# A decoder kernel on one core: a new order for the end of the last batch, a bank and a signal for each slot tile of an expert, and final sums on two engines

## The chip, the core and the metric

The kernel runs on one core of one Trainium2 chip. A core has five engines that each work through their own list of instructions in order and wait for one another by semaphores: TensorE (PE) for matmuls and transposes, VectorE (DVE), ScalarE (ACT), GpSimd (POOL), and SyncE (SP), which here only issues transfers. POOL issues the indirect (scatter) transfers. The metric is the device time of one execution in microseconds (us), as the median of the runs.

## The reference

Everything is float32. The input is x of 4 batches x 512 tokens x 128 features. One decoder layer is computed, with a layer norm after each of three parts:

```
# 1. gated delta net (8 heads, key and value width 128), then a small MLP
q, k = l2norm(silu(h Wq)), l2norm(silu(h Wk));  v = silu(h Wv);  h = rms_norm(x)
S = S * alpha_t ;  S = S + k_t (v_t - k_t S) beta_t ;  o_t = q_t S * scale   # over the 512 tokens
x1 = x + (rms_norm(o) * w * silu(h Wg)) Wo
a  = layernorm(x + x1 + relu(rms_norm(x1) W_fc)^2 W_proj)
# 2. attention of every token to 8 fixed rows of the context
x2 = layernorm(a + attention(a, ctx))
# 3. mixture of 8 experts, 2 for each token, at most 320 tokens to an expert, in token order
gates = softmax(x2 router_w + router_b);  idx = top 2;  pos = cumsum(mask) - 1;  valid = pos < 320
y = sum over the chosen experts of gate * (gelu(x2 w1[e] + b1[e]) w2[e] + b2[e])
out = layernorm(x2 + y)
```

## The kernel before

**Stages.** A prologue loads weights and prepares the keys of batch 0. Then each batch b of 0 to 3 goes through `levels(b)`, eight calls of `step(b, s)` and `between(b)`, which every engine has in its own version. The 512 tokens are four chunks of 128, and the 8 heads are two groups of four, so a batch has 8 units, n = 0 to 7. The recurrence is done in chunk form, for which a triangular system has to be inverted for each chunk and head. `between(b)` holds that inversion for batch b + 1: DVE eliminates 32 x 32 blocks in 31 dependent stages (`eliminate`, lines 1828 to 1860), with two places in it for other work (`aside(18)` and `aside(24)`, lines 1890 to 1896). The blocks then go out to memory and come back in another layout, by transfers on SP (`exchange_t`), and `levels` joins them into 128 x 128 blocks with small matmuls.

**The scan.** `step(b, s)` runs unit s of batch b: TT times v (`scan_tr`, PE), a copy on ACT, the products with the state (`scan_ks`, `scan_qs`, `scan_au`, `scan_ktu`), then on DVE `out_sum` (output of the unit), `state`, `out_norm` (its squared sum), then a power on POOL (`out_power`, line 493), then `gate_out` on DVE one step later (line 1701), and from it `out_transpose` and `out_proj` on PE, which give the residual. For b below 3 the same step prepares the keys of unit s + 2 of the next batch.

**Work of the batch before.** What follows the scan of a batch ("post" work) is cut into pieces: `post_x1`, `post_ssx`, `post_r1`, `post_m` (residual and its rms norm), `post_mT`, `post_fc`, `post_relu2`, `post_y` (MLP), `post_a_stats`, `post_rs1`, `post_a` (norm), `post_aT`, `post_sc`, `post_scores`, `post_sexp`, `post_probs`, `post_pT`, `post_xo` (attention), `post_x2_stats`, `post_rs2`, `post_x2` (norm), `post_x2T`, `post_lg`, `post_logits`, `post_lexp`, `post_choice`, `post_cum`, `post_slots` (router: a slot number for each token and choice), and `post_scatter` (POOL: 2 indirect transfers for each chunk of 128 tokens, line 587). The first ones up to `post_a` stand in `between(b)`; `post_aT` stands in `levels(b + 1)`, the rest in the steps of batch b + 1, and the scatters of batch b, 8 transfers, in POOL's `between(b + 1)`, between the power of the value norms (`rn`, line 547: 128 x 32 elements) and `post_r1(b + 1)`. The order of all of it is written out by hand in each engine's `step`, `post_piece` and `between`.

**The last batch** is split in two parts of two chunks each, FIRST and LAST. FIRST starts in step 5 of batch 3; LAST follows the last unit. The two are interleaved by hand in the branch `if kb >= B` of each engine's `between`. On DVE that is lines 1865 to 1886, on PE 949 to 966, on ACT 1408 to 1419.

**The gates** of the batch after next are 21 small dependent DVE operations on 128 x 32 elements (`gate_op`, lines 1605 to 1646). 3 of them stand early in step 6, the other 18 at its end (line 1801).

**Experts** (lines 1222 to 1240 on PE). SP loads the 320 slots of each expert as three tiles of 128, 128 and 64 rows (SLOT_TILES). For expert e PE transposes the rows, does the first product (4 matmuls into 4 banks), and the second (4 matmuls for each slot tile), with all three tiles in one PSUM bank, 5 or 6 by turns. ACT does the GELU. DVE waits for all three tiles, adds the bias b2, then multiplies by the gate (lines 2144 to 2153); POOL then adds the rows to memory with three accumulating indirect transfers (line 617), into `y_rows` for even experts and `out` for odd ones.

**Final norm** (lines 2155 to 2176). Two transfers for each batch bring both sums in; DVE adds them and takes the statistics, POOL takes the power, DVE the shift, and ACT writes the normalised rows, four instructions for each batch. Two sets of statistics are used by turns, so that DVE's `bn_aggr` of batch i waits for ACT to be done with batch i - 2 (`f_y`).

## Time and profile before

| | |
|---|---|
| median of 3 runs | 739.68 us (737.93 to 739.82) |
| profiled execution, its own time | 743.6 us |
| its span | 741.8 us |
| mean granted PE clock | 0.917 of full speed |
| batches 0 to 3 with what is between them | from 80 to 612 us of the span |
| rest of the last batch | 612 to 660 us |
| experts | 661 to 723 us |
| final norm | 724 to 742 us |

A line of a timeline has the start and the duration in us, engine, line, operation, the tiles written and read, the number of instructions that were merged, and in brackets how long the engine had been idle before and what released it. "issue" means that the profile shows no releaser. Line 470 is a helper for all powers with exponent -0.5, line 632 one for all transposes, line 667 one for products by heads, line 1247 one for copies on ACT; there the tile tells which piece it is.

### The profile page before, as it was taken

Reading aid. Unit: us, or ns where it says so; the run is one execution under the profiler, and the core shown is the slowest. Engines: PE = TensorE matmul, PEld = TensorE weight load, DVE = VectorE, ACT = ScalarE, POOL = GpSimd, SP = SyncE. Lnnn points to the kernel's source line nnn. Section 1 sums busy time; section 2 is a strip of 40 time slices with the busy share of each in tenths; the row PEclk is TensorE's granted clock in tenths of the full one; section 3 lists DMA queues with packets and bytes.
Section 4 is the critical chain, followed back from the end, with each engine's and each line's share of the span. In section 5 each row is a group of like instructions: output and inputs, shape, how many; then the busy total and the mean of one; then the engine's idle time right before and its main releaser. Section 6 shows DMA issues by size and latency. Waiting matters only on the chain.

```text
span 741.8 us, 14897 instructions
## 1 busy us (share of the span) xinstructions
PE 615.9 (83%) x5455; PEld 502.9 (68%) x5455; DVE 478.4 (64%) x1860; ACT 408.4 (55%) x723; POOL 268.4 (36%) x231
## 2 busy tenths in 40 slices
PE   2889899999998999999789999897888977329940
PEld 1466777888777777787577778785877865217730
DVE  4748834687797578887775687767857863522314
ACT  2735537887664687774455878655354643104413
POOL 3445003442362145316321433263212251224772
PEclk9999969999999999999899999998999995659985
DMA  7302220002005000200150002000502420022253
GB/s 250 138 10 63 77 33 1 2 1 50 24 26 98 2 1 15 44 15 16 38 101 3 1 15 44 15 13 27 102 2 58 155 65 10 10 48 45 21 83 113
DMA packets 78385, 34.04 MB, mean 46 GB/s; under 512 B 49969, under 2 KB 73850, under 8 KB 78185
## 3 DMA queue, kind: packets, MB, share of 16 engines
q1 hardware_dynamic: 74344, 30.89, 16.5%
q0 software_dynamic: 3968, 2.20, 2.2%
q8 instruction: 44, 0.72, 0.4%
q14 instruction: 29, 0.23, 0.1%
HBM read 20.04 MB, written 14.40 MB: 46 GB/s over the span
## 4 chain that ended last, share of the span: by engine, by line
PE 46%; DVE 18%; issue 14%; POOL 8%; ACT 7%; DMA 4%; SPq 1%; POOLq 0%; ACTq 0%; DVEq 0%
PE ps L667 16%; PE ps L632 5%; PE ps L709 4%; POOL slots L587 4%; PE ps L732 3%; DVE prod L1844 3%; DVE blk_t L1851 3%; PE ps L1035 2%; PE ps L821 2%; PE ps L809 2%; POOL y_rows L617 2%; POOL out L617 1%; PE ps L1014 1%; PE ps L1117 1%; DVE uo L1705 1%
## 5 line engine op out<-in xcount | busy, mean ns | idle before, releaser
L489 POOL TENSOR_TENSOR att<-att,br 128x512 f32<-128x512 f32 x32 | 33.2, 1042 | 183.9 <-ACT att L1301 175.5
L470 POOL TENSOR_TENSOR of<-oss,mhalf 128x4 f32<-128x4 f32 x32 | 32.5, 1017 | 111.2 <-DVE oss L1742 111.0
L470 POOL TENSOR_TENSOR st<-st,mhalf 128x4 f32<-128x4 f32 (+1 forms) x23 | 23.0, 1000 | 118.4 <-DVE st L1960 77.5
L1844 DVE TENSOR_TENSOR prod<-kn,blk_t 128x126 f32<-128x126 f32 (+35 forms) x244 | 54.7, 267 | 1.1 <-DMA kn<-n_blocks 1.1
L1851 DVE TENSOR_TENSOR blk_t<-blk_t,prod 128x126 f32<-128x126 f32 (+35 forms) x244 | 51.4, 254 | 0.1
L1247 ACT ACTIVATE ogT<-ps 128x512 f32<-128x512 f32 x32 | 19.1, 596 | 53.3 <-PE ps L632 53.3
L1247 ACT ACTIVATE uo<-ps 128x512 f32<-128x512 f32 x56 | 33.7, 602 | 25.9 <-PE ps L667 23.4
L1705 DVE SCALAR_TENSOR_TENSOR uo<-uo,of,gate_sb 128x128 f32<-128x128 f32 x128 | 40.4, 378 | 5.6 <-POOL of L470 5.6
L667 PEld LDWEIGHTS ps<-kT 128*128 128x128 f32 x256 | 32.6, 191 | 14.9 <-issue 14.6
L667 PE MATMUL ps<-qT,kT 128*128 128x128 f32 x256 | 40.1, 309 | 0.4 <-DVE att L1747 0.4
L928 PEld LDWEIGHTS ps<-ones,kT 128*128 128x128 f32 x256 | 32.7, 192 | 11.5 <-issue 10.5
L709 PE MATMUL ps<-w_qkvg,hT 128*128 128x512 f32 x64 | 38.4, 684 | 1.5 <-ACT kn L1283 1.5
L667 PEld LDWEIGHTS ps<-uo,att 128*128 128x128 f32 x256 | 32.9, 193 | 9.5 <-issue 9.2
L667 PE MATMUL ps<-vv,TT 128*128 128x128 f32 x256 | 35.6, 284 | 4.5 <-ACT TT L1452 4.3
L821 PEld LDWEIGHTS ps<-w_o,ogT 128*128 128x128 f32 x256 | 31.9, 196 | 10.8 <-ACT ogT L1247 9.5
L667 PEld LDWEIGHTS ps<-vv,TT 128*128 128x128 f32 x256 | 32.8, 198 | 8.7 <-issue 8.6
L907 PE MATMUL ps<-hT,w_qkvg 128*128 128x128 f32 x256 | 36.7, 289 | 1.6 <-DVE Nm L1690 0.9
L821 PE MATMUL ps<-w_o,ogT 128*128 128x128 f32 x256 | 36.0, 285 | 1.7 <-ACT ogT L1247 1.3
L587 POOL DMA_INDIRECT slots<-x_rows,scat_i x28 | 31.8, 1135 | 15.0 <-DVE scat_i L2100 7.6
L482 POOL TENSOR_TENSOR att<-const,g_all 128x512 f32<-128x512 f32 x32 | 33.0, 1040 | 9.1 <-DVE g_all L1643 9.1
L907 PEld LDWEIGHTS ps<-hT,w_qkvg 128*128 128x128 f32 x256 | 32.8, 201 | 4.7 <-ACT qT L1390 3.6
L667 PE MATMUL ps<-kT 128*128 128x128 f32 x256 | 34.4, 277 | 1.7 <-DVE Nm L1690 1.5
(251 smaller groups left out, 1738.5 us busy)
## 6 DMA issues: line engine op xcount, KB each, us to landing
tt_blocks<-gate_sb SPq DMA_DIRECT2D x4, 512.0 KB, 2.8
TT<-tt_blocks SPq DMA_DIRECT2D x16, 128.0 KB, 2.4
Nm<-in_L_ffn_w SPq DMA_DIRECT2D x1, 2048.0 KB
kn<-in_L_ffn_w SPq DMA_DIRECT2D x8, 256.0 KB
n_blocks<-Nm SPq DMA_DIRECT2D x16, 96.0 KB, 2.6
kn<-n_blocks SPq DMA_DIRECT2D x4, 384.0 KB, 3.4
t_blocks<-blk_t SPq DMA_DIRECT2D x4, 384.0 KB, 2.3
slots<-qT SPq DMA_DIRECT2D x5, 274.0 KB, 3.6
```

The lines of the kernel that those rows point to most:

```text
L470: pool.tensor_tensor(out_ap, in_ap, mhalf[:, 0:n], ALU.pow).then_inc(done, 1)
L489: pool.tensor_tensor(heads(att[:, slot(kb, m)]), heads(att[:, slot(kb, m)]), bc(br[:, kb % 2, unit(m)].unsqueeze(2), [P, HG, P]), ALU.mult ...
L587: pool.indirect_dma_start(slots_dram, bass.IndirectOffsetOnAxis(ap=scat_i[:, k, c:c + 1], axis=0), x2_of(q)[:, c - parts[q][1], :], None, ...
L632: return nc.tensor.transpose(out_ap, in_ap, ident[0:n, 0:n])
L667: last = mm(ps[bank][:, hs(h)], lhs(h), rhs(h), start=True, stop=True)
L709: mm(ps[KS][:], hT[:, kb % 3, c * P:(c + 1) * P], w_qkvg[:, 1, g * 512:(g + 1) * 512], start=True, stop=True).then_inc(sm["k_ps"], 1)
L821: last = mm(ps[HP][:, c * P:(c + 1) * P], ogT[:, n % 2, hs(h)], w_o[:, hh, :], start=(hh == 0), stop=(hh == H - 1), skip_group_check=True)
L907: last = mm(ps[KT][:, hs(h)], w_qkvg[:, 0, hh:hh + P], hT[:, kb % 3, c * P:(c + 1) * P], start=True, stop=True)
L1247: A(out_ap, in_ap, ACT.Copy).then_inc(done, 1)
L1705: last = stt(o_sb[:, n % 2, hs(h)], o_sb[:, n % 2, hs(h)], of[:, n * HG + h:n * HG + h + 1], gate_sb[:, n % 2, hs(h)], ALU.mult, ALU.mult)
L1844: counts.append(st.step(tt(pr, bc(bn_[:, j, i0:i0 + n].unsqueeze(2), [P, n, ncol]), bc(blk_t[:, j, 0:ncol].unsqueeze(1), [P, n, ncol]), AL ...
L1851: last = tt(rows_t, rows_t, pr, ALU.subtract)
```

## The change

- Between scans: POOL's `rn` power goes from `between` to the end of step 6 (`norm_power`), and the two scatters of the first chunk go to step 7, ahead of `out_power(b, 7)`, for batches 1 and 2. Six scatters stay where they were.
- Gate operations 9 to 20 go from the end of step 6 to step 7, behind `gate_out(b, 6)` and ahead of `out_sum(b, 7)`.
- `post_slots` is cut in two: `post_places` (it reads the PSUM bank) and `post_slots` (the rest, with fewer dependent operations: the test against the capacity, the product by 2 * SLOTS and the conversion to integers are fused; the running base is updated last). In batches 1 and 2 the second part stands behind `out_sum(b, 7)`. POST falls from 22 to 20. `cum_ok` now counts two signals for each part.
- On PE `post_pT` (step 1) and `post_x2T` (step 3) go behind `scan_ks`, `scan_qs`, `k_transpose` and `decay`; `post_y(b)` goes behind `head_eg` and `q_sums(kb, 7)`.
- Last batch: the first pieces of LAST (`post_mT`, `post_fc`, `post_m`) now come between those of FIRST, and `out_transpose(b, 7)` and `out_proj(b, 7)` ahead of the attention of FIRST; `post_y(FIRST)` goes behind `scan_au(7)`, `post_a(FIRST)` and `post_aT(FIRST)` go to `between`, `post_probs(LAST)` ahead of the slots of FIRST; the last sum of `post_cum(LAST)` is left out.
- Experts: each slot tile has a bank of its own (5, 6, 7) and a signal of its own, from PE to DVE, from DVE to POOL and back to PE. DVE writes bias times gate into the tile beforehand; one operation then does result times gate plus that.
- Final norm: the sums of batches 2 and 3 are done by POOL (`final_sum`), ahead of the powers of batches 0 and 1.

The core of the diff:

```diff
@@ POOL step / between / end
+                if 1 <= b < B - 1 and s == NU - 1:
+                    post_scatter(b - 1, 0)
                 if b >= 0 and s >= 0:
                     out_power(b, s)
+                if b >= 0 and kb < B and s == NU - 2:
+                    norm_power(kb)
...
+            def norm_power(kb):
+                pool.wait_ge(sm["kse_ok"], kb + 1)
+                if kb >= 1:
+                    pool.wait_ge(*after("vs_ok", kb - 1, NU, NU - 1))
+                pool.tensor_tensor(rn[:], rn[:], phalf[:], ALU.pow).then_inc(sm["rn_ok"], 1)
...
                 if b >= 1:
-                    for c in range(CH):
+                    for c in range(1, CH):
                         post_scatter(b - 1, c)
...
-                pool.wait_ge(sm["e_o_ok"], e + 1)
                 for t, (r0, n) in enumerate(SLOT_TILES):
+                    pool.wait_ge(*after("e_o_ok", e, len(SLOT_TILES), t))
...
+            def final_sum(i):
+                pool.wait_ge(*final_loaded(i))
+                pool.tensor_tensor(yf[:, i], yf[:, i], yo[:, i], ALU.add).then_inc(sm["sum_ok"], 1)
             for i in range(B):
+                if i < 2:
+                    final_sum(2 + i)
@@ PE between(3)
-                    post_sc(FIRST)
-                    out_transpose(b, NU - 1)
-                    out_proj(b, NU - 1)
-                    post_pT(FIRST)
-                    post_xo(FIRST)
-                    post_mT(LAST)
-                    for f in range(FC):
-                        post_fc(LAST, f)
-                    post_x2T(FIRST)
-                    post_y(LAST)
+                    out_transpose(b, NU - 1)
+                    post_aT(FIRST)
+                    out_proj(b, NU - 1)
+                    post_sc(FIRST)
+                    post_mT(LAST)
+                    post_fc(LAST, 0)
+                    post_fc(LAST, 1)
+                    post_pT(FIRST)
+                    post_fc(LAST, 2)
+                    post_fc(LAST, 3)
+                    post_xo(FIRST)
+                    post_y(LAST)
+                    post_x2T(FIRST)
@@ PE experts
-                if e >= 2:
-                    pe.wait_ge(sm["e_o_ok"], e - 1)
                 for t, (r0, n) in enumerate(SLOT_TILES):
+                    if e >= 1:
+                        pe.wait_ge(*after("e_o_ok", e - 1, len(SLOT_TILES), t))
...
-                        last = mm(ps[5 + a][0:n, t * P:(t + 1) * P], hidT[:, a, f, r0:r0 + n],
+                        last = mm(ps[5 + t][0:n, 0:P], hidT[:, a, f, r0:r0 + n], moe_w2[:, e, f, :],
...
+                    last.then_inc(sm["e_o_ps"], 1)
@@ ACT between(3)
-                    post_sexp(FIRST)
                     out_T(b, NU - 1)
+                    post_aT(FIRST)
+                    post_sexp(FIRST)
...
+                    post_aT(LAST)
                     post_lexp(FIRST)
@@ DVE step
+                if nxt and s == NU - 1:
+                    for i in range(GATE_SPLIT, GATE_OPS):
+                        gate_op(kb + 1, i)
                 if scan:
                     out_sum(b, s)
+                    if old and key and s == NU - 1:
+                        post_slots(b - 1)
@@ DVE between(3)
                     gate_out(b, NU - 1)
-                    post_scores(FIRST)
+                    post_a(FIRST)
                     post_x1(LAST)
                     post_ssx(LAST)
+                    post_scores(FIRST)
+                    post_m(LAST)
                     post_probs(FIRST)
...
                     post_scores(LAST)
+                    post_probs(LAST)
+                    post_places(FIRST)
                     post_slots(FIRST)
@@ DVE post_slots
-                ts(pairs(q, 12), pairs(q, 11), float(CAP), None, ALU.is_lt)
-                st.then(ts(pairs(q, 12, 2), pairs(q, 3), float(CAP), None, ALU.mult))
-                tt(pairs(q, 13), pairs(q, 11), pairs(q, 12, 2), ALU.add)
-                st.then(ts(pairs(q, 13, 1), pairs(q, 12), float(-2 * SLOTS), float(2 * SLOTS), ALU.mult, ALU.add))
-                st.then(tt(pairs(q, 13, 2), pairs(q, 13), pairs(q, 13, 1), ALU.add))
+                ts(pairs(q, 12), pairs(q, 11), float(CAP), float(2 * SLOTS), ALU.is_ge, ALU.mult)
+                st.then(stt(pairs(q, 13), pairs(q, 3), float(CAP), pairs(q, 11), ALU.mult, ALU.add))
+                tt(scat_i[:, :, span(q, 1)], pairs(q, 13), pairs(q, 12), ALU.add).then_inc(sm["slots_ok"], 1)
@@ DVE experts
-                    last = tt(oe[0:n, a, t, :], ps[5 + a][0:n, t * P:(t + 1) * P], moe_b2[0:n, e * P:(e + 1) * P], ALU.add)
+                    last = ts(oe[0:n, a, t, :], moe_b2[0:n, e * P:(e + 1) * P], wgt_e[0:n, e, t:t + 1], None, ALU.mult)
...
+                    dve.wait_ge(*after("e_o_ps", e, len(SLOT_TILES), t))
+                    stt(oe[0:n, a, t, :], ps[5 + t][0:n, 0:P], wgt_e[0:n, e, t:t + 1], oe[0:n, a, t, :],
+                        ALU.mult, ALU.add).then_inc(sm["e_o_ok"], 1)
```

## Rows read from the trace of the kernel before

**Rows 1.** Page, part 1: busy us, share of span, instructions of each engine.

```profile
PE 615.9 (83%) x5455; PEld 502.9 (68%) x5455; DVE 478.4 (64%) x1860; ACT 408.4 (55%) x723; POOL 268.4 (36%) x231
```

**Rows 2.** Waits of PE: engine, line <- releaser: us in total, times, longest.

```profile
PE ps L632 <- DVE uo L1705: 9.7, 7, 2.2
PE ps L632 <- DVE x L2020: 9.4, 5, 3.2
...
PE ps L632 <- DVE x_rows L1964: 5.6, 4, 3.0
```

**Rows 3.** Timeline, batch 1, end of the scan: start, us, engine, line, operation [idle before].

```profile
328.04 0.18 DVE L1623 TENSOR_SCALAR gates<-gates 128x32 f32<-128x32 f32 x1
...
334.26 1.13 DVE L1705 SCALAR_TENSOR_TENSOR uo<-uo,of,gate_sb 128x128 f32<-128x128 f32 x4
...
335.45 0.66 PE L632 MATMUL ps<-const,uo 128*128 128x128 f32 x4 [2.06 <-DVE uo L1705]
```

**Rows 4.** Timeline, between batches 1 and 2.

```profile
339.23 5.43 POOL L547 TENSOR_TENSOR rn<-rn,phalf 128x32 f32<-128x32 f32 x1
...
341.23 0.32 DVE L1844 TENSOR_TENSOR prod<-kn,blk_t 128x45 f32<-128x45 f32 x2
...
349.13 0.69 DVE L1972 TENSOR_TENSOR x<-xr,ps 128x512 f32<-128x512 f32 x1 [3.27 <-PE ps L821]
...
356.97 1.06 POOL L470 TENSOR_TENSOR st<-st,mhalf 128x4 f32<-128x4 f32 x1
...
358.06 1.41 DVE L1985 TENSOR_SCALAR a<-x,st 128x128 f32<-128x128 f32 x4 [4.50 <-POOL st L470]
```

**Rows 5.** Instructions of line 587: count: ns min/median/max, first and last start.

```profile
L587 POOL DMA_INDIRECT slots<-x_rows,scat_i x28: 964/972/2084, 344.8 to 659.1; - x28
```

**Rows 6.** Timeline, between batches 2 and 3.

```profile
497.05 0.69 DVE L1972 TENSOR_TENSOR x<-xr,ps 128x512 f32<-128x512 f32 x1 [3.04 <-PE ps L821]
...
505.96 1.41 DVE L1985 TENSOR_SCALAR a<-x,st 128x128 f32<-128x128 f32 x4 [4.49 <-POOL st L470]
```

**Rows 7.** Timeline, end of the elimination and start of the levels, ahead of batches 1 and 2.

```profile
223.59 1.89 DVE L1747 TENSOR_TENSOR att<-ps,att 128x512 f32<-128x512 f32 x3
...
229.54 2.21 PE L1014 MATMUL ps<-uo,Nm 32*32 32x32 f32 x128 [1.13 <-DMA uo<-t_blocks]
...
372.76 1.89 DVE L1747 TENSOR_TENSOR att<-ps,att 128x512 f32<-128x512 f32 x3
...
380.79 2.21 PE L1014 MATMUL ps<-uo,Nm 32*32 32x32 f32 x128 [0.87 <-DVE att L1747]
```

**Rows 8.** Timeline, last scan step of batch 3 and the work behind it.

```profile
606.40 1.12 DVE L1716 SCALAR_TENSOR_TENSOR uo<-uo,eg,ps 128x128 f32<-128x128 f32 x4 [2.22 <-PE ps L667]
...
612.14 0.69 PE L632 MATMUL ps<-const,a 128*128 128x128 f32 x2 [3.50 <-DVE a L1964]
...
618.69 0.42 DVE L1972 TENSOR_TENSOR x<-xr,ps 128x256 f32<-128x256 f32 x1 [3.05 <-PE ps L821]
...
637.19 0.17 DVE L2077 SCALAR_TENSOR_TENSOR rt<-ps,base 128x16 f32<-128x16 f32 x1 [0.50 <-PE ps L1171]
...
639.24 0.34 DVE L2018 TENSOR_REDUCE rt<-x 128x16 f32<-128x192 f32 x1
...
655.30 0.96 POOL L587 DMA_INDIRECT slots<-x_rows,scat_i  x1 [5.37 <-DVE scat_i L2100]
```

**Rows 9.** Timeline, experts 0 and 1.

```profile
670.40 3.07 PE L1238 MATMUL ps<-kn,att 128*128 128x128 f32 x24
...
675.81 1.58 POOL L617 DMA_INDIRECT y_rows<-kT,tok_e  x1 [15.71 <-DVE kT L2152]
...
681.67 1.55 POOL L617 DMA_INDIRECT out<-kT,tok_e  x1 [0.67 <-issue]
```

**Rows 10.** Page, part 5, one group; then the timeline of the final norm.

```profile
L489 POOL TENSOR_TENSOR att<-att,br 128x512 f32<-128x512 f32 x32 | 33.2, 1042 | 183.9 <-ACT att L1301 175.5
...
735.19 0.38 DVE L2167 BATCH_NORM_AGGREGATE rt<-bn 128x2 f32<-128x6 f32 x4 [0.28 <-ACT vv L1561]
```

121 lines of the change are left out of this document (61 added, 60 removed).

## Prediction

> **What bounds the kernel now.** I read the page's busy shares first, then the chain of waits, then PE's waits, and then the timeline of every place that the change touches. PE is busy 83% of the span and no other engine over 64% [rows 1]. So in the scans what counts is PE's idle time, and the wait that ends last; outside them the bound changes. There are four places:
>
> - End of a scan. In batch 1 DVE does gate operations from 328.04 on and then the slots, and only at 334.26 `gate_out` of unit 6, although POOL's power for it was done at 329.2. PE stands 2.06 us for it [rows 3].
> - Between batches. DVE's elimination is the long chain. In it DVE stands 3.27 us for the residual (PE's `out_proj(7)`) and 4.50 us for `post_m`, whose power on POOL starts at 356.97, behind the `rn` power of 5.43 us and eight scatters [rows 4]. Between batches 2 and 3 the same stands are 3.04 and 4.49 us [rows 6].
> - Last batch. From 606 to 655 us one short dependent operation follows another over all engines [rows 8].
> - Experts and end. After the first expert, POOL's groups of scatters start 5.86 us apart [rows 9], at PE's pace (4 first products, 3 transposes, 12 second products, with PE busy throughout). The final norm goes at ACT's pace [rows 10].
>
> **The change part by part.** Times are those of the profiled execution, 743.6 us (span 741.8). The median of the runs is 739.68, 3.9 us less; I take the sum off both alike.
>
> *1. Gates and slots behind `gate_out(6)`.* The 18 gate operations at the end of step 6 and the slots take 334.26 - 328.04 = 6.2 us [rows 3]. After the change only 6 gate operations (1.4 us) and the two reads of `post_places` (0.4) stand ahead of `gate_out(6)`, so it starts at about 329.9 and PE's stand of 2.06 us goes. Behind it stand 12 gate operations (12 x 0.22 = 2.65) ahead of `out_sum(7)`, which by that comes at 333.5, not later than PE's product for it. Over all places PE waits 9.7 us in 7 stands for this operation [rows 2]; the one of batch 0, which has gates but no slots, I take at 1.0.
>
> *2. Between batches 1 and 2.* PE comes 2.06 us earlier to `out_proj(7)`, so DVE's stand at the residual shrinks by that. The `rn` power goes into step 7, where POOL is idle. Scatters take 0.97 us, with 0.3 between them, at times 2.08 [rows 5]; six instead of eight remain, and they start at about 340 instead of 344.8, so POOL is free at about 349.9. The sums of squares are then there at 349.0, `post_m`'s power ends at 351.0, and DVE comes to `post_m` at 353.56 - 2.06 = 351.5: the 4.50 goes whole. The elimination ends 6.56 us earlier. Before, the levels of batch 1 started 229.54 - 223.59 = 5.95 us after it, released by the transfers, but those of batch 2 only 380.79 - 372.76 = 8.03 after it, released by DVE's `att` product, which was late because PE had stood for `post_mT` as well [rows 7]. With that stand gone the transfers decide here too: 2.08 more. Together 8.6; the least is 4.5, if PE is late anyway.
>
> What this adds: two scatters ahead of `out_power(7)`. Slot numbers come at about 335.7, the first scatter 0.85 later, the second is done 2.4 after its start, so the power starts at 339.1, not 336.8 as it could, and `gate_out(7)` and the elimination come 0.7 later than before. DVE's stand of 3.27 - 2.06 = 1.2 us at the residual covers it. Between 2 and 3 the same pair costs 2.6 and the cover is 3.04 [rows 6]; above 3.04 it goes onto the elimination one for one.
>
> *3. Between batches 2 and 3.* No gates there and no stand of PE at unit 6, so only the 4.49: 4.5. `post_y` behind `head_eg` and `q_sums(7)` fills a stand of PE for ACT and I count it at nothing; without that it would delay `post_a_stats` by at most 1.5, which `att` products hide.
>
> *4. Steps 1 and 3.* PE stands 9.4 us in 5 places for the probabilities and 5.6 in 4 for x2 [rows 2]. Two of the first kind (batches 1, 2) are 1.33 each and two of the second 1.02, together 4.7, and PE gets about 1.7 us of key work to do in each. But ACT keeps its order and so copies the keys after `post_pT`: `kT_copy` comes 0.7 us later than before. The whole 4.7 comes only if the keys have that slack. Bounds 0 and 5.6; I take 3.0.
>
> *5. Last batch.* `post_y(FIRST)` behind `scan_au(7)`: `out_sum(7)` at 604.6 instead of 606.40, with `post_a_stats` (1.3) no longer ahead of `out_norm(7)`. PE's transposes of FIRST at 612.14, after 3.5 us idle, no longer stand ahead of unit 7 [rows 8]. Step by step (power 1.0, `gate_out` 1.1, transposes 0.5, copy 0.6, products 1.15) the residual of LAST comes at 612.7 instead of 618.69: 6.0. Then: the transposes of LAST are no longer behind the attention of FIRST (-1.1 at `post_y`); `post_a_stats(LAST)` waits for `post_x2(FIRST)` on DVE (+1.0); `post_a(LAST)` waits for the logits of FIRST (+0.6); `post_lexp(FIRST)` behind `post_aT(LAST)` on ACT makes `post_choice(FIRST)` late and it holds `post_scores(LAST)` (+1.4). So scores come 4.1 earlier. The slots of FIRST, 639.24 - 637.19 = 2.05 us [rows 8], no longer stand ahead of `post_probs(LAST)`: 6.1. Last, one product less in `post_cum` (0.45) and slots of 1.2 us instead of 2.1 (0.9): 7.4. POOL is idle 5.37 us before LAST's scatters [rows 8], so they simply follow. I take 7.0 for one small miss. Bounds 3.4 (the slots' reorder and the shorter slots alone) and 9 (PE at its full clock through this stretch, where it now works at half, after having idled).
>
> *6. Experts.* The second product of expert 0 starts at 670.40 and takes 3.07; POOL's first scatter starts at 675.81 [rows 9], 5.4 after it. With a signal for each tile: 4 of 12 matmuls (1.0), one DVE operation (0.3), POOL's start (0.85): 2.2. So 3.2 earlier. After that POOL's own pace (3 transfers, 5.5 us) and PE's (5.77) stay as they were, and the end moves by the same 3.2. Bounds 2.5 and 3.6.
>
> *7. Final norm.* `bn_aggr` of batch 2 waits for ACT [rows 10], so the two sums on DVE (0.68 each) lie beside ACT's work: removing them gives nothing. On POOL such an operation takes 1.04 [rows 10], ahead of the power of batch 0, and the transfers of batch 2 land last: -0.5, bounds 0 and -2.
>
> Sum: 1.0 + 8.6 + 4.5 + 3.0 + 7.0 + 3.2 - 0.5 = 26.8. 743.6 - 26.8 = 716.8 for an execution like the profiled one, and 739.7 - 26.8 = 712.9 for the median. Added waits are one for each slot tile (PE on DVE's read of the same bank one expert before, 4.8 us earlier in time, so nothing stands behind it), and DVE's wait for the scatter of two experts before, now ahead of the bank's read.
>
> A rule that speaks against part 2: the Trainium skill, page "SBUF — State Buffer", section "SBUF: two separate sides", says that a GpSimd operation and a VectorE operation with two SBUF inputs exclude each other for a whole instruction. The trace disagrees for this power: DVE's products of the elimination, with two inputs, run under it at 0.32 us for a pair [rows 4]. What it would do is rival C.
>
> **The rivals.**
> A. The gain between batches is absorbed: the scatter pair and the longer path to `gate_out(7)` eat the cover, or the levels are held by PE or ACT instead of by the transfers. For it: covers of 1.2 and 3.04 against 0.7 and 2.6 are thin. Against: the 4.5 us stands have nothing else in them. It takes 9 of the 16.1 in parts 2 to 4: 722.
> B. More goes: PE's clock stays up between batches and in the last batch, and steps 1 and 3 give all. 1.7 + 2 + 2 + 1.3 more: 706.
> C. The `rn` power locks DVE out in step 7: `gate_out(6)`, ready at 329.9, waits until 334.6, where it was before, with 3.8 us now behind it, in three batches: 3 x 4.7 = 14.1 lost: 727.
> D. Slower. The loop over the experts turns into a chain: the bank of expert e is read only when the scatter of e - 2 has landed, and PE can be one expert ahead instead of two. A landing takes about 4.0 us from the last scatter's start; the loop of 5.5 + 4.0 + 2.2 for two experts fits in 11.5. From there each us more costs 0.5 us for each expert, and PE idles and falls to half its clock, at which the 12 products take 6 us and the period 11 instead of 5.8: 7 x 5 = 35 lost, 748. It needs landings nearly twice as long.
> E. The change does what it says but only the end counts (parts 5 to 7): 9.7 gained: 730.
>
> **How the numbers follow.** Forecast 0.60, with its own range 707 to 719; A 0.16, B 0.12, C 0.04, E 0.04, D 0.04. Range 702 to 726: it leaves out C, D and E and the far side of B. Runs of this kernel lie within 0.3%, 2 us, which is what a measurement can tell from no change. All but D lie far below it: faster 0.95, same 0.02, slower 0.03.
>
> **What would show it.** Part 1: the transposes of unit 6 in batch 1 without a wait. Parts 2 and 3: DVE's stands at lines of `post_m` gone in both, that at `post_x1` near 0.3 us, and the levels released by the transfers. Part 5: residual of LAST about 6 us nearer to the first residual work, last scatter right behind it. Part 6: 2.2 us from product to scatter, period 5.8. Part 7: ACT with a gap before each batch's rows. I am wrong if `gate_out(7)` comes more than 3 us later after unit 7's norm, or if a new stand of DVE in the elimination appears.

## Result and the profile after

| | before | after |
|---|---|---|
| median, us (range, runs) | 739.75 (737.93 to 741.92, 4) | 712.66 (711.54 to 713.62, 4) |
| ratio, 95% interval | | 0.9632 [0.9601, 0.9664] |
| profiled execution: span, us | 741.8 | 711.7 |

Medians and ranges in this document are over all executions, and ratios leave out those in a slower state of the chip, which two of e10's six were in.

Forecast was 712.9 (702 to 726). The sum was right, but several of its terms were not, and it was luck that their errors cancelled. This is read by stages. Their borders are the starts of POOL's powers of the unit norms (`of<-oss`), of the last slot numbers (`scat_i`), and of the first and last scatter of the experts. "Clock" is the length of the stage times (1 - its mean granted clock), in us. A low clock costs nothing while PE is idle, so this is the most that it can have taken. A stand is idle time in which an engine waits for another. In the column of the forecast the step of the prediction is in brackets.

| stage | before | after | change | forecast | clock before/after |
|---|---|---|---|---|---|
| start to unit 0 of batch 0 | 126.50 | 125.46 | -1.04 | 0 | 10.2/8.5 |
| to unit 0 of batch 1 | 135.02 | 132.78 | -2.24 | -1.0 (step 1) | 3.4/3.4 |
| batch 1, unit 0 to 6 | 66.68 | 63.70 | -2.98 | -1.5 (step 4) | 0/0 |
| to unit 0 of batch 2 | 83.55 | 74.91 | -8.64 | -8.6 (step 2) | 5.1/5.1 |
| batch 2, unit 0 to 6 | 66.76 | 63.97 | -2.79 | -1.5 (step 4) | 0/0 |
| to unit 0 of batch 3 | 72.41 | 68.48 | -3.93 | -4.5 (step 3) | 5.1/3.4 |
| batch 3, unit 0 to 6 | 51.01 | 47.77 | -3.24 | 0 | 0/0 |
| to the last slot numbers | 52.37 | 46.89 | -5.48 | -7.0 (step 5) | 18.1/15.4 |
| to the experts' first scatter | 21.51 | 19.41 | -2.10 | -3.2 (step 6) | 7.5/8.5 |
| to their last | 43.83 | 43.76 | -0.07 | 0 | 1.3/0 |
| to the end | 22.16 | 24.57 | +2.41 | +0.5 (step 7) | 11.1/11.5 |
| sum | 741.8 | 711.7 | -30.1 | -26.8 | |

The page of the changed kernel, busy times and the chain that ended last by engine:

```profile
PE 611.8 (86%) x5453; PEld 503.3 (71%) x5453; DVE 477.3 (67%) x1841; ACT 407.3 (57%) x723; POOL 285.2 (40%) x233
PE 64%; DVE 17%; ACT 6%; issue 5%; DMA 5%; POOL 1%; SPq 1%; ACTq 0%; DVEq 0%; POOLq 0%
```

PE has the same work as in [rows 1] in a shorter span, and POOL has all but left the chain (1%, before 8%). PE's waits after (columns as in [rows 2]): of the four stands for `x_rows` only the longest is left, in the last batch, and those for x fell from 9.4 to 1.5. The levels' wait for the transfers (L1030) rose from 3.7 us in two places to 7.8 in three:

```profile
PE ps L646 <- DVE uo L1724: 9.0, 6, 2.7
PE ps L1030 <- DMA uo<-t_blocks: 7.8, 3, 3.2
PE ps L646 <- DVE x_rows L1990: 3.0, 1, 3.0
PE ps L646 <- DVE x L2046: 1.5, 2, 1.0
```

End of batch 1's scan and what follows, timelines of VectorE with PE's transposes of unit 6, and of POOL:

```profile
323.26 0.18 DVE L2109 TENSOR_REDUCE rt<-ps 128x8 f32<-128x32 f32 x1
323.36 0.87 DVE L1724 SCALAR_TENSOR_TENSOR uo<-uo,of,gate_sb 128x128 f32<-128x128 f32 x3
...
326.96 0.60 PE L646 MATMUL ps<-const,uo 128*128 128x128 f32 x4
...
333.93 1.14 DVE L1724 SCALAR_TENSOR_TENSOR uo<-uo,of,gate_sb 128x128 f32<-128x128 f32 x4 [3.70 <-POOL of L471]
...
340.59 0.69 DVE L1998 TENSOR_TENSOR x<-xr,ps 128x512 f32<-128x512 f32 x1
...
344.97 0.86 DVE L2011 TENSOR_SCALAR a<-x,st 128x128 f32<-128x128 f32 x4
```

```profile
322.92 5.42 POOL L538 TENSOR_TENSOR rn<-rn,phalf 128x32 f32<-128x32 f32 x1
330.33 1.20 POOL L595 DMA_INDIRECT slots<-x_rows,scat_i  x1 [1.99 <-DVE scat_i L2127]
331.83 0.99 POOL L595 DMA_INDIRECT slots<-x_rows,scat_i  x1 [0.30 <-issue]
332.83 1.06 POOL L471 TENSOR_TENSOR of<-oss,mhalf 128x4 f32<-128x4 f32 x1
...
342.81 1.04 POOL L471 TENSOR_TENSOR st<-st,mhalf 128x4 f32<-128x4 f32 x1 [0.20 <-DVE st L2004]
```

`gate_out(6)` (323.36) follows the two reads of the slots at once, and PE transposes its result (326.96) without a stand, where it had waited 2.06 us. The residual (340.59) and `post_m` (344.97) have no idle time ahead of them: both stands of [rows 4] are gone. POOL finishes its last scatter 0.2 us before the residual's sums are there. The pair of scatters in step 7 (330.33, 331.83) delays `out_power(7)` (332.83), as forecast: it comes 10.9 us after unit 6's power instead of 10.0, and in batch 2 10.5 instead of 7.9.

The levels ahead of batches 2 and 3, PE, and the granted clock there (by windows: PEclk is the number ahead of the DMA share):

```profile
366.20 2.48 PE L1030 MATMUL ps<-uo,Nm 32*32 32x32 f32 x128 [1.80 <-DVE att L1766]
504.32 3.57 PE L1030 MATMUL ps<-uo,Nm 32*32 32x32 f32 x128 [3.18 <-DMA uo<-t_blocks]
```

```profile
500.00:504.00 4.00, 1.13 (x11) 0.94 (x9) 3.90 (x13) 0.00 (x0) 2.03 (x3) 1.00 0.50 153
504.00:508.00 4.00, 3.68 (x129) 3.62 (x130) 3.20 (x7) 0.66 (x2) 1.99 (x2) 0.55 1.19 166
508.00:512.00 4.00, 4.00 (x108) 3.66 (x108) 1.32 (x2) 1.11 (x2) 0.00 (x0) 0.59 0.22 42
```

Ahead of batch 3, PE has run out of work, is busy 1.13 of 4 us, and does the levels at half its clock (0.55). Ahead of batch 2 it stands 1.80 us. There the clock had already fallen once before, from 357.7 to 361.1, with no idle time of PE in the 12 us before, but with matmuls on few columns (128x1 and 128x32) just ahead. `post_y` ran in that time and came late, and by it `att`, which releases the levels.

The last step of batch 3, in order PE, ACT, VectorE:

```profile
579.10 1.16 PE L681 MATMUL ps<-uo,att 128*128 128x128 f32 x8
580.09 1.95 PE L1133 MATMUL ps<-w_pr,att 128*128 128x128 f32 x16
581.88 0.60 PE L646 MATMUL ps<-const,uo 128*128 128x128 f32 x4
582.52 0.60 ACT L1264 ACTIVATE ogT<-ps 128x512 f32<-128x512 f32 x1 [2.69 <-PE ps L646]
583.66 0.69 DVE L1758 TENSOR_REDUCE oss<-ogT 128x4 f32<-128x512 f32 x1 [2.25 <-ACT ogT L1365]
585.80 1.14 DVE L1724 SCALAR_TENSOR_TENSOR uo<-uo,of,gate_sb 128x128 f32<-128x128 f32 x4
590.91 0.42 DVE L1998 TENSOR_TENSOR x<-xr,ps 128x256 f32<-128x256 f32 x1 [3.45 <-PE ps L834]
```

`post_y` (L1133) no longer stands ahead of unit 7's product, but it stands ahead of unit 6's transposes. ACT copies those before it squares unit 7, so VectorE waits 2.25 us for the square. Behind `gate_out(7)` (585.80) the residual of LAST (590.91) comes 4.0 us after its end.

Experts, and the final norm (POOL, then VectorE):

```profile
635.57 4.64 PE L1245 MATMUL ps<-kT,Nm 128*128 128x320 f32 x8 [0.53 <-ACT kT L1264]
640.86 3.10 PE L1255 MATMUL ps<-kn,att 128*128 128x128 f32 x24
643.90 2.42 PE L1245 MATMUL ps<-kT,Nm 128*128 128x320 f32 x8
643.37 1.58 POOL L625 DMA_INDIRECT y_rows<-kT,tok_e  x1 [13.61 <-DVE kT L2182]
```

```profile
696.78 1.26 POOL L631 TENSOR_TENSOR vv<-vv 128x512 f32<-128x512 f32 x1 [8.23 <-DMA vv<-out]
698.14 1.42 POOL L471 TENSOR_TENSOR st<-st,mhalf 128x4 f32<-128x4 f32 x1
699.55 1.25 POOL L631 TENSOR_TENSOR vv<-vv 128x512 f32<-128x512 f32 x1
696.48 0.38 DVE L2200 BATCH_NORM_AGGREGATE rt<-bn 128x2 f32<-128x6 f32 x4
696.89 1.17 DVE L2202 TENSOR_SCALAR st<-rt 128x4 f32<-128x4 f32 x1
699.60 0.38 DVE L2200 BATCH_NORM_AGGREGATE rt<-bn 128x2 f32<-128x6 f32 x4
700.01 0.82 DVE L2202 TENSOR_SCALAR st<-rt 128x4 f32<-128x4 f32 x1
```

From the product (640.86) to the scatter (643.37) it is 2.5 us, before 5.4. In the final norm two operations of VectorE that took 0.17 us before take 1.17 and 0.82, and end with POOL's two sums (698.04, 700.80).

### The profile page after: what moved, and what is told of

Same layout as the page of the kernel before. It is cut to its first block, busy times and chain, and to the rows that moved or that the text cites. A ratio compares the mean times of both kernels' runs of the same rounds, so it can differ in the third digit from the quotient of the medians.

```text
span 711.7 us, 14886 instructions
## 1 busy us (share of the span) xinstructions
PE 611.8 (86%) x5453; PEld 503.3 (71%) x5453; DVE 477.3 (67%) x1841; ACT 407.3 (57%) x723; POOL 285.2 (40%) x233
## 4 chain that ended last, share of the span: by engine, by line
PE 64%; DVE 17%; ACT 6%; issue 5%; DMA 5%; POOL 1%; SPq 1%; ACTq 0%; DVEq 0%; POOLq 0%
PE ps L681 21%; PE ps L646 6%; PE ps L722 4%; DVE blk_t L1874 4%; DVE prod L1867 4%; PE ps L834 4%; PE ps L1255 3%; PE ps L745 3%; PE ps L822 3%; PE ps L1245 3%; PE ps L1051 2%; PE ps L920 2%; PE ps L930 2%; PE ps L1030 2%; PE ps L941 2%
## 5 line engine op out<-in xcount | busy, mean ns | idle before, releaser
L1867 DVE TENSOR_TENSOR prod<-kn,blk_t 128x126 f32<-128x126 f32 (+35 forms) x244 | 51.9, 251 | 1.2 <-DMA kn<-n_blocks 1.2
L681 PE MATMUL ps<-qT,kT 128*128 128x128 f32 x256 | 41.6, 317 | 0.4 <-DVE att L1766 0.4
L941 PEld LDWEIGHTS ps<-ones,kT 128*128 128x128 f32 x256 | 32.6, 192 | 11.5 <-issue 10.8
L681 PEld LDWEIGHTS ps<-qT,kT 128*128 128x128 f32 x256 | 36.4, 221 | 1.0 <-issue 0.4
L920 PE MATMUL ps<-hT,w_qkvg 128*128 128x128 f32 x256 | 34.9, 279 | 1.6 <-DVE Nm L1709 0.9
L1758 DVE TENSOR_REDUCE oss<-ogT 128x4 f32<-128x512 f32 x32 | 21.9, 683 | 21.1 <-ACT ogT L1365 20.9
```

The costliest lines, as they stand in the source:

```text
L681: last = mm(ps[bank][:, hs(h)], lhs(h), rhs(h), start=True, stop=True)
L920: last = mm(ps[KT][:, hs(h)], w_qkvg[:, 0, hh:hh + P], hT[:, kb % 3, c * P:(c + 1) * P], start=True, stop=True)
L941: last = mm(ps[KS][:, n * HG + h:n * HG + h + 1], qsq(kb, n)[:, hs(h)], ones[:, 0:1], start=True, stop=True, skip_group_check=True)
L1867: counts.append(st.step(tt(pr, bc(bn_[:, j, i0:i0 + n].unsqueeze(2), [P, n, ncol]), bc(blk_t[:, j, 0:ncol].unsqueeze(1), [P, n, ncol]), AL ...
```

## Experiments

Each run is the changed kernel with one edit, if not said otherwise; in the code `...` stands for lines left out. Executions of one kernel differ by 2 to 9 us (e10: 13), and the medians of the kernel before by 2.5 between the groups of runs: it took 741.3 beside e5 to e8, 1.6 more than in the table above, so their medians overstate their losses by about that. Each ratio is against the kernel before, run beside it; that of the changed kernel is 0.9632. Small effects are read from the stages of the profiled executions, "x against y" being the edited against the changed kernel. Each kernel has one such profile. Units 0 to 6, where no edit touches them, mostly repeat to 0.1 us and vary by at most 0.9, and the other stages vary with the clock: start to unit 0 lay between 123.6 and 126.3, and the stage to the last slot numbers, in kernels without an edit in it, between 44.6 and 46.9.

**e1: final sums on VectorE.**

```diff
-                if i < 2:
-                    final_sum(2 + i)
...
-                        dve.wait_ge(sm["sum_ok"], i - 1)
+                    dve.wait_ge(*final_loaded(i))
+                    st.then(tt(yf[:, i], yf[:, i], yo[:, i], ALU.add))
...
```

> The changed kernel with all four final sums on VectorE again; nothing else differs. Theory (lock): in the changed kernel two VectorE operations with one input each, at 0.17 us before, take 1.17 and 0.82 us and end within 0.03 us of POOL's two sums, and batch 0's power starts 0.99 us later, behind the sum. From the first landed sum to the end of the span it takes 16.9 us, in the kernel before 15.2. So taking the sums off POOL gives 1.6 us: 711.0 us, and 0.17 us for each of the four operations. Rival (hidden, as my prediction had it at 0.5): VectorE's sums cost what POOL's cost: 712.7 to 712.2. Rival (landing): the 0.7 us by which the last loads land later after the last scatter are the cost, and stay: no more than 0.9 gained.

710.82 us, ratio 0.9609 [0.9571, 0.9646]. The interval overlaps that of the changed kernel, so the profile decides. From the start of the first sum to the end of the span it takes 15.2 us against 16.9, as the lock theory said (in the four profiles with this edit it is 15.2, in the nine without it 16.7 to 17.0). The operations take 0.17 again:

```profile
697.56 0.38 DVE L2191 BATCH_NORM_AGGREGATE rt<-bn 128x2 f32<-128x6 f32 x4
697.98 0.17 DVE L2193 TENSOR_SCALAR st<-rt 128x4 f32<-128x4 f32 x1
```

The landing (last scatter to first sum) is not part of it: 6.9 us before, 7.7 after, 8.3 here, 6.8 to 8.1 in other runs.

**e2: `post_y(FIRST)` later in the last step.**

```diff
-                if kb >= B and s == 7:
-                    post_y(FIRST)
...
                     post_fc(FIRST, 2)
                     post_fc(FIRST, 3)
+                if kb >= B and s == 7:
+                    post_y(FIRST)
...
```

> The changed kernel with PE's post_y(FIRST) in the last step behind out_transpose(6), gate_proj(7) and out_proj(6) instead of ahead of them, post_aT(FIRST) behind out_proj(7), and VectorE's post_a_stats(FIRST) behind gate_out(7). Theory: in the changed kernel the 16 matmuls of post_y (1.95 us) stand ahead of out_transpose(6), by that ACT copies ogT only at 582.52 and squares unit 7 only after it, and VectorE stands 2.25 us for the square. With y behind, the norm of unit 7 comes some 2 us earlier, gate_out(7) at about 583.5 instead of 585.8, the residual of LAST 2.3 earlier, and the end 2.0 to 2.5 earlier: 710.4 us. Rival (FIRST decides): what is late next is the attention of FIRST, whose a1 comes no earlier, and post_choice(FIRST) holds post_scores(LAST): 712.7, within 0.5 us of the changed kernel. Rival (clock): PE works at 0.67 of its clock here either way; y ends later and post_a_stats(FIRST) now holds VectorE: 713.5.

712.57 us, ratio 0.9639 [0.9599, 0.9678]: no gain in the median. In the profile the mechanism is there: VectorE's stand for the square is 0.70 instead of 2.25, unit 6 to the residual of LAST takes 10.9 us against 13.8, and to the last slot numbers 44.4 against 46.9. But the clock took 2.7 us less in that stage too, and e7, without the edit, had 44.6 there. The mechanism is shown; whether the order gains time stays open.

**e3: orders of the last batch as before.** PE's order behind the scan, the others alike:

```diff
+                    post_sc(FIRST)
                     out_transpose(b, NU - 1)
-                    post_aT(FIRST)
                     out_proj(b, NU - 1)
-                    post_sc(FIRST)
+                    post_pT(FIRST)
+                    post_xo(FIRST)
                     post_mT(LAST)
...
```

> The changed kernel with the orders of the last batch of PE, ACT and VectorE as they were before (post_y, post_a_stats and post_a of FIRST in step 7, FIRST ahead of LAST behind it, slots of FIRST ahead of post_probs(LAST)); the shorter slots and the product less in post_cum stay. Prediction's term: 5.7 of its 7.0 us (6.1 for the order, less 0.4 of the allowance for a miss): 718.4 us. Theory from the trace of after: the residual of LAST moved by 2.9 relative to unit 6, scores gave back 0.9, the slots' place gave 2.1, so the order is worth 4.2: 716.9 us. Rival: the order gives nothing beyond the slots' place: 714.8.

718.16 us, ratio 0.9709 [0.9673, 0.9745]. The stage to the last slot numbers is 50.55 against 46.89, 3.7 more, with the clock equal (15.5 against 15.4 taken). The residual of LAST comes 17.0 us after unit 6 against 13.8. In the profile the trace's 4.2 is nearer than my term's 5.7; the median lies 5.5 higher, and its interval holds both. The third case, that the order gives nothing, is refuted.

**e4: one signal for three slot tiles.**

```diff
-                    pool.wait_ge(*after("e_o_ok", e, len(SLOT_TILES), t))
+                    pool.wait_ge(*after("e_o_ok", e, len(SLOT_TILES), len(SLOT_TILES) - 1))
...
-                    dve.wait_ge(*after("e_o_ps", e, len(SLOT_TILES), t))
+                    dve.wait_ge(*after("e_o_ps", e, len(SLOT_TILES), len(SLOT_TILES) - 1))
```

> The changed kernel in which VectorE waits for all three slot tiles' second products before its first operation, and POOL for all three of VectorE's; banks and the merged VectorE operation stay. Theory: product to first scatter takes 2.51 us in the changed kernel; with one signal it waits for the end of 12 products (3.1) plus three operations (0.9) plus POOL's start (0.85): 4.9, so 2.4 later for all scatters: 715.1 us; the period of 5.77 stays, since PE sets it. Rival (merge): the gain of 2.9 came from merging two VectorE operations and preparing the bias ahead; the signals give under 0.5: 713.0. Rival (absorbed): POOL's three scatters (5.5) in a period of 5.77 catch up 0.27 for each expert, so of 2.4 only 0.5 are left after seven experts: 713.2.

714.54 us, ratio 0.9663 [0.9628, 0.9699]. From the second product to the first scatter it takes 4.9 us against 2.5, as the theory said, and from the last slot numbers to the experts' first scatter 21.35 against 19.41, so 1.9; the period stays (43.76 from the first scatter to the last). By the profile both rivals fell; the medians alone (1.9 apart, with intervals that overlap) could not tell. The signals are two thirds of the 2.9 us that signals and merge gave in step 6.

**e5: the `rn` power back between batches.**

```diff
-                if b >= 0 and kb < B and s == NU - 2:
-                    norm_power(kb)
...
-                if b < 0:
-                    norm_power(kb)
+                norm_power(kb)
```

> The changed kernel with the `rn` power (5.42 us on POOL) back behind out_power(7), ahead of the scatters between batches; the first pair of scatters stays in step 7. Prediction's working: POOL comes free 5.4 later, post_m's stand is back with about 4.9 between 1 and 2 and between 2 and 3, and the levels of batch 2 are held by att again (2.1): 11.9 lost, 724.6. Theory from the trace of after (no slack left: residual's power at 342.81, 0.2 after its input, right behind the scatters, post_m at 344.97 without a stand): 5.4 less 1.3 of slack for each place, 8.2 to 10.8 lost, 721 to 723.5. Rival (the gain came from elsewhere, the x1 stand): under 4 lost, 716. Rival (lock): the rn power slows VectorE in step 7, and without it there gate operations and gate_out(6) come sooner: 1 to 2 us given back, 719 to 721, and gate_out(6) of batch 1 before 323.3 on the changed kernel's scale.

722.77 us, ratio 0.9764 [0.9678, 0.9851]. Between 1 and 2: 81.72 against 74.91, between 2 and 3: 73.99 against 68.48, together 12.3, of which up to 6.8 is more clock lost. The median lies 10.1 higher, by the ratios 9.8: the theory from the trace (8.2 to 10.8 lost). The stand is back:

```profile
346.60 1.41 DVE L2008 TENSOR_SCALAR a<-x,st 128x128 f32<-128x128 f32 x4 [3.91 <-POOL st L471]
```

Step 7 of the scan takes as long with the power in it as without it: unit 0 to unit 7 of batch 1 is 74.6 us in both. So the power locks nobody out in step 7.

**e6: all eight scatters between batches.**

```diff
-                if 1 <= b < B - 1 and s == NU - 1:
-                    post_scatter(b - 1, 0)
...
-                    for c in range(1, CH):
+                    for c in range(CH):
```

> The changed kernel with all eight scatters of a batch between the batches (the first pair out of step 7); the `rn` power stays in step 7. Prediction's working: the pair costs gate_out(7) 0.7 between 1 and 2 and 2.6 between 2 and 3, under covers of 1.2 and 3.04 at the residual; back between the batches it puts two scatters (2.5 us) ahead of the residual's power, which has at most 2.5 of slack: nothing, 712.7. Theory from the trace of after: the residual has no stand of VectorE at all in after, so the cover is gone and gate_out(7) is on the elimination's chain: the pair's removal gives 0.7 to 1 in the scan and takes up to 1.2 at post_m (slack 1.3 of 2.5): within 1 us of the changed kernel, 711.9 to 713.5; in the trace of this kernel out_power(7) of batch 1 starts 0.7 or more earlier, and post_m stands by about 1. Rival (pair essential): POOL's chain had no slack: 2.5 lost at two places, 717.5.

720.79 us, ratio 0.9744 [0.967, 0.9819]: above all forecasts, 3.3 us above the last rival, and not by its mechanism, since POOL was done with its scatters when the residual's sums came. `out_power(7)` comes 2.5 us sooner, as expected, and PE's `out_proj(7)` sets the residual. But the residual starts 2.9 us after PE's product for it has ended (338.37), and ACT's next operation 2.1 after its own:

```profile
337.31 1.06 PE L832 MATMUL ps<-w_o,ogT 128*128 128x128 f32 x8
338.20 1.06 PE L918 MATMUL ps<-hT,w_qkvg 128*128 128x128 f32 x8
341.25 0.69 DVE L1996 TENSOR_TENSOR x<-xr,ps 128x512 f32<-128x512 f32 x1 [5.49 <-remote]
341.35 0.60 ACT L1403 ACTIVATE qT<-ps 128x512 f32<-128x512 f32 x1 [2.73 <-remote]
```

The profile names no releaser ("remote"). Between 1 and 2 it is 3.3 us longer (78.23 against 74.91), with the clock equal. The second place is 7.7 us longer (76.16 against 68.48), up to 6.8 of it clock, in the levels of batch 3:

```profile
510.00:515.00 5.00, 5.00 (x112) 4.61 (x109) 2.93 (x6) 1.46 (x3) 0.49 (x1) 0.50 0.55 105
515.00:520.00 5.00, 5.00 (x165) 4.65 (x159) 2.08 (x4) 0.61 (x2) 0.00 (x0) 0.50 0.02 3
520.00:525.00 5.00, 5.00 (x37) 4.78 (x38) 2.04 (x3) 1.16 (x2) 0.00 (x0) 0.50 0.00 0
```

All four executions lie between 719.95 and 723.1, so the loss isn't the chance of one. What delays the two engines stays open. With all of the clock taken off, 4.2 us are lost in the two places, and the late residual (2.9 us later after unit 6's power in each) is more than that, so what the pair itself is worth can't be told from this run.

**e7: gates and slots ahead of `gate_out(6)`.**

```diff
-            GATE_SPLIT = 9
+            GATE_SPLIT = GATE_OPS
...
-                    if old and key and s == NU - 1:
-                        post_slots(b - 1)
...
                     post_places(b - 1)
+                    post_slots(b - 1)
```

> The changed kernel with all 18 gate operations at the end of step 6 and post_slots right behind post_places, ahead of gate_out(6). Prediction's working: PE's stand of 2.06 for gate_out(6) is back in batch 1 and 1.0 in batch 0, and the slots of batch 2 (1.3 us) stand ahead of gate_out(6) there: 3.1 to 3.6 lost, 716. Theory from the trace of after: batch 0's unit 7 moved by 0.3 only, batch 1's stand of 2.06 is gone, and scatters for which POOL has room start earlier: 2.5 lost, 715.2. Rival (cover): the elimination had 1.2 of cover left at the residual and takes it: 1 lost, 713.7.

717.57 us, ratio 0.969 [0.9617, 0.9763]. To batch 1: 135.33 against 132.78; between 1 and 2: 79.03 against 74.91; between 2 and 3: 0.4 more. Together 7.0, up to 3.4 of it clock; the last batch then is 2.3 shorter, with 4.4 less clock lost. With the clock taken off it is 3.6, at the upper end of my working's 3.1 to 3.6. Such late `remote` releases are here too, on ACT (4.60 us idle at 344.16, 4.31 at 485.31); the first delays PE's product for the residual by only 0.3, since other products stand ahead of it.

**e8: PE's `post_pT` and `post_x2T` early in steps 1 and 3.**

```diff
-                if old and s not in (1, 3):
+                if old:
                     post_piece(b, s)
...
-                if old and s in (1, 3):
-                    post_piece(b, s)
```

> The changed kernel with PE's post_pT in step 1 and post_x2T in step 3 ahead of scan_qs, kt and the decays again, as before. Prediction's term: 3.0 (2 x (1.33 + 1.02), less what ACT's order gives back): 715.7. Theory from the milestones of after (POOL's powers of the unit norms): unit 1 gains 1.7, 1.5 and 1.6 us in batches 1, 2 and 3, units 3 and 4 gain 1.2, 1.3 and 0.7 more, and nothing is given back by unit 6: 7.5 to 9 lost, 720.2 to 721.7; my term left batch 3 out and took the stands for the whole price. Rival (ACT): keys late by 0.7 for each place give half back: 3 to 4 lost, 716.

725.79 us, ratio 0.9812 [0.9721, 0.9903]. Units 0 to 6 take 66.46, 66.74 and 50.12 against 63.70, 63.97 and 47.77: 2.76, 2.77 and 2.35, with no clock in it. So the two moves give 7.9 us in the scans alone. Between 1 and 2 it is 4.8 longer as well, up to 3.4 of it clock. Late releases as in e6 are here too: the residual comes 2.4 us later after unit 6's power between 1 and 2, and 2.1 between 2 and 3. So the median, 4 us above the theory, holds more than the two moves, and only the scans price them.

**e9: filler matmuls ahead of the experts**, with e1's edit and ACT's `post_lexp(FIRST)` ahead of `post_aT(LAST)`.

```diff
+            def fill(n):
+                for _ in range(n):
+                    mm(ps[QSG][:], ident, w_qkvg[:, 3, 0:512], start=True, stop=True)
...
             pe.wait_ge(sm["e_w"], 16 * (E + 2))
+            fill(14)
             expert_rows(0)
...
```

> The changed kernel with three edits: final sums on VectorE (worth 1.7 from the first landed sum to the end in the run before), ACT's post_lexp(FIRST) ahead of post_aT(LAST), and 14 matmuls of 128x512 whose result nobody reads, on PE while it waits 11.28 us for the slots' rows. Theory (clock): in the changed kernel PE enters the experts at half its clock, after that wait: the first transposes take 0.96 us for three (0.59 later), the first products 4.64 us for eight (2.42 later), so with PE kept busy the first scatter of the experts comes 2.6 to 3 us earlier after the last scatter of the slots; and ACT's edit lets post_scores(LAST) start about 0.9 sooner, since VectorE stood 1.05 us for that exponential. Sum 1.7 + 2.8 + 0.9: 707.3 us. Rival (clock not the cause): the slow first products are bound by ACT's table load and its activations (4 x 1.07), so the filler gives at most 0.5: 709.5. Rival (filler in the way): it ends behind the landing of the rows and costs up to 1: 711.

712.88 us, ratio 0.9626 [0.9583, 0.9669]. The filler took 14.5 us (the profile shows two matmuls for each of its 14), and PE came to the rows 4.4 us late: my third case, and more than it said. But the first products behind it took 2.42 us for eight instead of 4.64. So the clock is the cause of their length, and not ACT; what that gains was hidden here.

**e10: e9 with three more in each of two stands of the last batch.**

```diff
-                    for stage in (post_pT, post_xo, post_x2T, post_lg, post_cum):
+                    for stage, n in ((post_pT, 0), (post_xo, 0), (post_x2T, 3), (post_lg, 0), (post_cum, 3)):
+                        fill(n)
```

> As the kernel with 14 unread matmuls, with three more ahead of post_x2T(LAST) and three ahead of post_cum(LAST), where PE stands 3.04 and 2.92 us. Theory (clock): PE works at half clock through this stretch; if the six bring it to the full one, its 12 short steps from there to the last scatter's numbers (some 5 us of matmuls at half clock) take half: 1 to 2 us less: 705.8. Rival (in the way): at half clock three take 3 us, as long as the stand, the clock stays where it is, nothing or 0.5 lost: 707.5.

710.89 us (704.38 to 717.33), ratio 0.9564 [0.9507, 0.962]. The executions that the ratio counts have a median of 707.9, which is nearer to the rival (707.5) than to the theory (705.8), but spread over 9 us. In the profile the theory holds: the stage to the last slot numbers took 43.6 against e9's 45.8, with 6.8 of clock lost instead of 14.7.

**e11: `post_y` between batches ahead of `head_eg` and `q_sums(7)`.**

```diff
                 q_sums(kb, 6)
+                if old:
+                    post_y(b)
                 if nxt:
                     head_eg(kb + 1)
                 q_sums(kb, 7)
-                if old:
-                    post_y(b)
```

> The changed kernel with PE's post_y between the batches ahead of head_eg and q_sums(7), as before. Prediction: nothing, as q_sums waits for ACT's square and fills no gap of the path; 712.7. Rival: post_y behind q_sums is what holds the levels of batch 2 now (released by VectorE's att, 7.1 us after the elimination, not 5.95, since post_a_stats stood 1.66 us for y): back in front it gives 1.1 between 1 and 2: 711.6. Rival: it costs what the reorder meant to give, up to 1.5 for each of three places: 715.

709.16 us, ratio 0.9583 [0.9539, 0.9627]. The interval overlaps that of the changed kernel, and 1.9 us of the profile's gain lie ahead of all edits; but to batch 1 it took 130.22 against 132.78, and between 1 and 2 72.92 against 74.91, with no clock lost in either (3.4 and 5.1 in the changed kernel). The other profiles show that this is not chance: the changed kernel, e1 to e4, e9 and e10, which are alike up to there, took 132.6 to 134.2 and 74.1 to 75.5, and e12, which has this edit too, took 130.5 and 72.2. PE's levels of batch 2 and the windows around them:

```profile
361.05 2.21 PE L1030 MATMUL ps<-uo,Nm 32*32 32x32 f32 x128 [1.56 <-DMA uo<-t_blocks]
```

```profile
355.00:360.00 5.00, 4.49 (x41) 4.29 (x39) 4.70 (x15) 3.21 (x3) 1.27 (x2) 1.00 0.60 168
360.00:365.00 5.00, 3.95 (x165) 3.74 (x168) 4.94 (x10) 1.35 (x3) 2.75 (x3) 1.00 1.08 145
```

PE waits 1.00 us for the input of `post_y` and only then does `q_sums(7)` and two grams, so it has work until shortly before the levels. Ahead of batches 1 and 2 the stand before the levels is 1.2 to 1.6 us in e11 and e12 and 0.9 to 1.1 in the kernel before, and the levels' first group of matmuls (L1030) takes 2.21 us in all six places. In the seven kernels with the other order the stand is 1.8 to 4.0 us and the group takes 2.4 to 3.6. Between 2 and 3 PE stands 2.3 us in e11, the group takes 3.5, and nothing changes (68.45 against 68.48).

**e12: a version that beats both**: e1's and e11's edits, ACT's order, and filler of 2, 3 and 8.

> The changed kernel with final sums on VectorE, ACT's post_lexp(FIRST) ahead of post_aT(LAST), post_y between batches back ahead of head_eg and q_sums(7), and unread matmuls sized to PE's stands: 2 ahead of post_x2T(LAST), 3 ahead of post_cum(LAST), and 8 ahead of the experts (16 passes; the 28 passes of the runs before took 14.5 and 12.3 us in a stand of 11, so they were 4.4 us too long). Theory: 1.7 for the sums and 2.0 for the exponential and the fuller clock up to the last slot numbers (both measured in the profiles of the runs before), and 2.9 from last scatter of the slots to first scatter of the experts (13.9 to 14.6 down to 11.7): 6.6 in all: 706.1 us; the place of post_y adds 0 to 2 of it. Rival (the landing of the slots' rows decides): with the transposes at full clock it still takes 10 us from the last numbers to the rows, so the experts gain 1.5 at most: 707.5. Rival (clock elsewhere): filler only moves where PE loses its clock, as the levels after each elimination lose 1.7 us more or less by chance: 709 to 711.

700.93 us (698.52 to 703.4), ratio 0.9488 [0.9451, 0.9526], 11.7 us below the changed kernel. By stages: to batch 1 -2.3, between 1 and 2 -2.8 (both `post_y`), last batch -1.5, to the experts' first scatter -3.2 (16.23 against 19.41), end -2.2. PE ahead of the experts:

```profile
618.13 8.83 PE L675 MATMUL ps<-w_qkvg,const 128*128 128x512 f32 x16 [1.38 <-DVE scat_i L2127]
627.73 0.64 PE L640 MATMUL ps<-const,qT 128*128 128x128 f32 x3 [0.77 <-DMA qT<-slots]
628.90 2.42 PE L1245 MATMUL ps<-kT,Nm 128*128 128x320 f32 x8 [0.53 <-ACT kT L1264]
```

The filler ends 0.8 us before the rows land, and the first products take 2.42 us instead of 4.64. It is more than my 6.6, by `post_y`, which I had put at 0 to 2 and which gave 5.1. By the ratios, each against the kernel before beside it, it is 0.0144 or 10.7 us below the changed kernel: 1 of the 11.7 lies in the group of runs.

## Why the prediction was right, step by step

1. *Gates and slots behind `gate_out(6)`*: right. PE's stand is gone; undone (e7) it costs 3.6 without the clock, and my terms gave 3.1 (to 3.6 with the slots of batch 2). In batch 0 the residual comes 1.2 us earlier after unit 6 (forecast 1.0); the rest of the 2.24 to batch 1 is no more than what this stage varies by.
2. *Between 1 and 2*: 8.6 forecast, 8.64 measured, and the stands went as the step said. Its last term failed: the levels of batch 2 start 7.1 us after the elimination, not 5.95, and are again released by `att`, since `post_a_stats` waits 1.66 us for `post_y`, which now stands later and ran at half the clock. (In e2, e4, e9 and e10, where the clock held under `post_y`, the transfers released the levels, as forecast, but the stage took 74.1 to 75.5 all the same.) But the elimination itself, counted from unit 6, ended 7.4 us earlier, not 6.56: in all it ended at 359.1 instead of 372.7, and 6.3 of that had been gained by unit 6. Of the surplus 0.55 is that the four operations of `post_m`, with no stand ahead, take 0.86 us instead of 1.41. So the sum held. The pair of scatters moved `out_power(7)` by 0.8 and 2.6 us (forecast 0.7 and 2.6), and the stands at the residual covered it: between 2 and 3 it comes 18.5 us after unit 6 before and after. Taking the pair out (e6) made things worse, by causes outside the sum.
3. *Between 2 and 3*: 4.5 forecast, 3.93 measured. The failed step is "I count it at nothing" for `post_y`: e11 and e12 show 2.0 to 2.8 us at two of three places. I asked who waits for `post_y`, not what its move leaves PE to do ahead of the levels. The gain comes in just the two stages in which the clock is regained. That the term is wrong is shown; that the clock is the whole of it is read from these profiles, not tested by itself.
4. *Steps 1 and 3*: the term most mis-sized, 3.0 forecast, 9.0 measured, 7.9 by e8. The stands of batch 3 were left out (2.35), though the edit holds there too, and the allowance for ACT's order, 1.7, was not needed: 2.8 for each batch is more than the stands of 1.33 and 1.02 together. What gives the 0.4 beyond the stands in each batch stays open.
5. *Last batch*: 7.0 forecast, 5.5 measured. Of the 6.0 at the residual of LAST 2.9 came. Up to unit 7's power only 0.2 came of 1.4, since `post_y` ahead of the transposes of unit 6 held VectorE by 2.25. I priced the transposes, the copy and the products behind `gate_out(7)` at 2.25 us, PE's full clock, though the products behind it took 2.07 us for eight there, against 1.06 in the scan; the three took 4.0. What followed was as said: scores lost 0.9 (1.9 forecast), the slots' place gave 2.1 (2.05), the shorter slots 0.9, the product less 0.4.
6. *Experts*: signals and merge gave 2.9 of 3.2; but the first products ran slower, 4.64 instead of 4.05, and took 0.8 back.
7. *Final norm*: 0.5 lost was forecast, within 0 to 2, and 2.4 measured: 0.7 a later landing that other runs show to vary, 1.7 the lock (e1), which the step did not have. It counted POOL's sum in front of the power, and not what it does to VectorE beside it.

Gains beyond the forecast of 6.0 (step 4), 1.2 (to batch 1) and 1.0 (ahead of all edits) met shortfalls of 0.6, 1.5, 1.1 and 1.9 (steps 3, 5, 6, 7), and the medians (-27.1) moved 3.0 less than the profiles (-30.1). So the forecast of 26.8 met the median's 27.1 in part by luck. The rivals: C is refuted for the power by e5, though the lock it speaks of appears in the sums of step 7; A and B each had a part (more in the scans, less elsewhere); the loop of D never closed (43.76 us from first to last scatter, before 43.83); E is refuted, since parts 5 to 7 gave 5.2 of the 30.1.

## What to carry to other kernels

Price a moved operation by what it leaves the engine to do in its old place too: here stands of PE of 1.8 to 4.0 us right ahead of the levels went with half the clock in them, and those of 0.9 to 1.6 did not, which is not seen in any wait. Count an edit in every iteration in which its condition holds. Where the sum is right, compare it stage by stage before believing its terms.
